# Two attentions on one core: GpSimd's third mask goes ahead of a subtraction, and the guarded add of the first attention moves into the next step

## The reference, cut to what matters

```
x = x + L0_attn(layernorm(x))            # 32 sequences of 256 tokens, 16 heads of 8, causal
x = x + L0_ffn(layernorm(x))             # routed experts
h = layernorm(x)                         # L1_attn, on the same tokens:
for l in range(4):
    xn = ln(h, ln1_w[l], ln1_b[l])
    q, k, v = heads(xn @ Wq.T + bq), heads(xn @ Wk.T + bk), heads(xn @ Wv.T + bv)
    scores = (q k^T + rel_shift((q + u) r^T)) * HEAD_DIM ** -0.5
    p = softmax(where(j > i, -inf, scores))
    h = h + (p v) @ Wo.T + bo
    h = h + gelu(ln(h) @ W1.T + b1) @ W2.T + b2
x = x + h
...                                      # top-2 experts, performer, fp4 feed-forward, one-head attention, adapters
```

## Time and profile before

| | |
|---|---|
| median of 3 runs | 6347.32 us (6344.32 to 6354.53) |
| profiled execution, its own time | 6347.19 us |
| its span | 6345.5 us |
| TensorE matmul, busy | 5660.9 us (89%) |
| VectorE, busy | 4069.9 us (64%) |
| ScalarE, busy | 2817.1 us (44%) |
| GpSimd, busy | 2118.2 us (33%) |

### The profile page before, as it was taken

The page is one execution under the profiler, slowest core; times in us unless marked ns, Lnnn a source line. Parts: engine busy times, 40 slices in busy tenths (PEclk is TensorE's granted clock), DMA queues, the critical chain, the costliest instruction groups (busy, mean ns, idle before and its releaser), DMA issues. The chain is left out here.

```text
span 6345.5 us, 121186 instructions
## 1 busy us (share of the span) xinstructions
PE 5660.9 (89%) x38029; PEld 3508.4 (55%) x38029; DVE 4069.9 (64%) x9572; ACT 2817.1 (44%) x4608; POOL 2118.2 (33%) x3000
## 2 busy tenths in 40 slices
PE   7997999999997999979987999889988989886677
PEld 5664444444443677457754777457754556644564
DVE  7885666666664777357744776367745756567854
ACT  4553222222221555535553555445554645543344
POOL 5551000000001666146632665156620012253322
PEclk9998999999998999989998999989999999997799
DMA  4332323222323555045522554055510000000002
GB/s 132 103 108 93 97 98 98 95 97 97 97 98 99 154 149 151 1 128 152 151 62 62 155 150 125 3 148 153 149 39 5 0 7 0 1 4 0 0 2 61
DMA packets 526328, 527.02 MB, mean 83 GB/s; under 512 B 55698, under 2 KB 436705, under 8 KB 503780
## 3 DMA queue, kind: packets, MB, share of 16 engines
q1 hardware_dynamic: 517684, 517.90, 29.3%
q10 hardware_dynamic: 8320, 5.25, 0.3%
HBM read 337.88 MB, written 185.07 MB: 82 GB/s over the span
## 5 line engine op out<-in xcount | busy, mean ns | idle before, releaser
L361 DVE TENSOR_REDUCE a_mx<-a_unit 128x2 f32<-128x512 f32 (+1 forms) x1920 | 1298.5, 688 | 611.7 <-PE a_unit L556 602.9
L460 ACT ACTIVATE a_prob<-a_slot 128x1536 f32<-128x1536 f32 x640 | 929.1, 1452 | 732.4 <-PE a_slot L579 577.7
L554 PE MATMUL a_unit<-a_sk,a_sq 96*128 96x256 bf16 (+3 forms) x5120 | 747.7, 250 | 87.9 <-DVE a_mx L361 44.3
L1169 ACT ACTIVATE f_silu<-f_pG 128x512 f32<-128x512 f32 x528 | 315.1, 598 | 934.4 <-PE f_pG L1244 920.4
L556 PE MATMUL a_unit<-a_maskq,identb 128*128 128x256 bf16 (+1 forms) x1920 | 602.5, 314 | 0.0
L1111 DVE TENSOR_TENSOR f_gated<-f_spread,f_silu 128x512 f32<-128x512 f32 x512 | 354.6, 693 | 348.2 <-ACT f_silu L1169 308.0
L1221 PE MATMUL f_pO<-f_hidden,f_wd 128*128 128x512 f32 x1056 | 545.0, 598 | 14.2 <-DVE f_hidden L1113 14.0
L554 PEld LDWEIGHTS a_unit<-a_sk,a_sq 96*128 96x128 bf16 (+1 forms) x5120 | 382.8, 99 | 291.2 <-DVE a_mx L361 161.3
L1244 PE MATMUL f_pG<-f_xnT,f_wg 128*128 128x512 f32 x1056 | 541.8, 595 | 0.0
L1248 PE MATMUL f_pU<-f_xnT,f_wu 128*128 128x512 f32 x1056 | 540.7, 594 | 0.0
L602 PE MATMUL a_pctx<-a_prob,a_vaug 128*32 128x256 f32 x5120 | 422.9, 391 | 90.9 <-POOL a_prob L307 86.7
(11 more groups left out here) (409 smaller groups left out, 11027.7 us busy)
## 6 DMA issues: line engine op xcount, KB each, us to landing
f_spread<-f_scratch SPq DMA_DIRECT2D x1024, 128.0 KB, 2.9
a_sq<-a_qscratch SPq DMA_DIRECT2D x128, 768.0 KB, 5.7
a_sk<-a_kscratch SPq DMA_DIRECT2D x160, 384.0 KB, 6.6
a_qscratch<-a_parts SPq DMA_DIRECT2D x288, 192.0 KB, 2.3
a_qscratch<-a_parts SPq DMA_DIRECT2D x288, 128.0 KB, 2.2
a_kscratch<-a_parts SPq DMA_DIRECT2D x160, 192.0 KB, 2.2
a_kscratch<-a_parts SPq DMA_DIRECT2D x160, 128.0 KB, 2.2
a_qscratch<-a_parts SPq DMA_DIRECT2D x288, 64.0 KB, 1.8
```

The costliest lines, as they stand in the source:

```text
L361: v.tensor_reduce(dst, src, op=ALU.max, axis=AX.X, negate=True).then_inc(red_done, 1)
L460: act.activation(prob[gr % 2][:, :], slot[:, :], ACT.Exp, scale=SCALE).then_inc(exp_done, 1)
L554: pe.matmul(bank[:, at * wide:(at + 1) * wide], q, sk[b][0:KM, gr * GH + h, 0:wide], start=(at == 0), stop=False)
L1169: act.activation(silu[c % 2][:, :], pG[c % 2][:, :], ACT.Silu).then_inc(silu_done, 1)
```

## The change

Three moves, none of which adds or removes work on data:

1. GpSimd, both attentions: the masks of the third head group (`causal(2)`) are issued between the first cast of the split and its subtraction, no longer between the subtraction and the second cast. One more semaphore increment (`apart`) stands in front of the subtraction.
2. GpSimd, first attention: the fill of `guard` goes from the start of the step to its end.
3. VectorE, first attention: the guarded add of sequence n-1 goes from the end of step n to step n+1, behind that step's fifth reduction (`units(3, 5)`), as `add_guarded(n - 2)`. The last one is done at the end of the last step.

```diff
@@ GpSimd
-                    if not rel and is_seq(n - 1):
-                        if is_seq(n - 2):
-                            g.wait_ge(op_taken, n - 1)
-                        g.tensor_tensor(guard[:, :, :], zeros[:, :, :], zeros[:, :, :], op=ALU.add).then_inc(guard_done, 1)
                     causal(0)
...
                         chain.link(g.tensor_copy(pt[:, :, 0, :], f32s[:, :, :]))
-                        chain.link(g.tensor_tensor(rest[:, :, :], f32s[:, :, :], pt[:, :, 0, :], op=ALU.subtract))
                     causal(2)
                     if is_seq(n + 4):
                         pt = parts[j % 2]
+                        g.sem_inc(apart, 1)
+                        chain.link(g.tensor_tensor(rest[:, :, :], f32s[:, :, :], pt[:, :, 0, :], op=ALU.subtract))
                         chain.link(g.tensor_copy(pt[:, :, 1, :], rest[:, :, :]))
                         g.tensor_tensor(pt[:, :, 2, :], rest[:, :, :], pt[:, :, 1, :], op=ALU.subtract
                                         ).then_inc(parts_done, 1)
+                    if not rel and is_seq(n - 1):
+                        if is_seq(n - 2):
+                            g.wait_ge(op_taken, n - 1)
+                        g.tensor_tensor(guard[:, :, :], zeros[:, :, :], zeros[:, :, :], op=ALU.add).then_inc(guard_done, 1)
@@ VectorE
+                def add_guarded(m):
+
+                    dst = rows(store, m * QT, QT)
+                    v.wait_ge(guard_done, m + 1)
+                    v.wait_ge(osb_done, m + 1)
+                    chain.link(v.tensor_tensor(isnum[:, :, :], osb[:, :, :], osb[:, :, :], op=ALU.is_equal))
+                    chain.link(v.copy_predicated(guard[:, :, :], isnum[:, :, :], osb[:, :, :]))
+                    v.tensor_tensor(dst, guard[:, :, :], dst, op=ALU.add).then_inc(op_taken, 1)
...
                     units(3, 5)
+                    if not rel and is_seq(n - 2):
+                        add_guarded(n - 2)
...
                     units(9, 12)
-                    if is_seq(n - 1):
+                    if rel and is_seq(n - 1):
                         dst = rows(store, (n - 1) * QT, QT)
-                        if rel:
-                            v.wait_ge(op_pe, n)
-                            got = ring[0][:, 0:SEQ].rearrange("p (t d) -> p t d", d=D)
-                        else:
-                            v.wait_ge(guard_done, n)
-                            v.wait_ge(osb_done, n)
-                            chain.link(v.tensor_tensor(isnum[:, :, :], osb[:, :, :], osb[:, :, :], op=ALU.is_equal))
-                            chain.link(v.copy_predicated(guard[:, :, :], isnum[:, :, :], osb[:, :, :]))
-                            got = guard[:, :, :]
+                        v.wait_ge(op_pe, n)
+                        got = ring[0][:, 0:SEQ].rearrange("p (t d) -> p t d", d=D)
                         v.tensor_tensor(dst, got, dst, op=ALU.add).then_inc(op_taken, 1)
+                    if not rel and once(n, SEQS):
+                        v.drain()
+                        add_guarded(n - 1)
```

## The result

The changed kernel takes 6261.98 us (median of 4 runs, 6256.44 to 6276.41) against 6347.75 of the kernel before, taken beside it: ratio 0.9873, 95% interval 0.986 to 0.9885. The forecast of 6286 had the sign and the main mechanism, and was 24 us too high. The profiled execution has a span of 6259.8 us.

The account below looks back on a forecast made before the run. TensorE was taken to set the pace in both attentions, so only its idle gaps could be won. From 6347.3, less 78 (relative attention) plus 17 (first attention), came 6286 us; range 6250 to 6338.

Parts of the forecast that it names:

- Relative attention, the wait for L307 gone: -78 us: Relative attention: TensorE's wait at values for GpSimd's second mask instruction goes, except in each layer's last four sequences; -78 us.
- L67 delayed to 1.8 us a pair, covered by 0.3 us: Relative attention: VectorE's L67 pair meets the moved subtraction, yet the reduction behind it is 0.3 us early; cost 0.
- Rivals 3 and 4: Relative attention: L67's second instruction waits for cast L336, 6336 us (12%); GpSimd starves VectorE, 6535 us (5%).
- SP's cover holds: Relative attention: SP's writes and loads behind `parts_done` still bring the stack in time for `maxima`; cover's thickness unknown.
- rival 5: Relative attention: a wait of `maxima` for the stack's loads replaces the one for L307; 6364 us, 6%.
- The added increment and the guard fill: 0: GpSimd: the extra semaphore increment costs next to nothing; first attention's guard fill goes to an idle stretch, 0 us.
- First attention, uncollided: -1 us, 0.52 of the 0.56 given back: First attention: without collision, the moved add ends one 0.56 us wait but delays L678, keeping 0.04 a step; -1 us.
- Collision: two of three instructions 0.33 us late each, +17 us: First attention: L432 and L434 of the moved add each meet a GpSimd mask, making L678 0.66 us later; +17 us.

Follow-up runs that it names:

- The add alone: The changed kernel with the old order on GpSimd, so only guard fill and guarded add are moved: 6340.31 us, ratio 0.9995 to the kernel before.

## Why the prediction was right, and where it was not

- *Relative attention, the wait for L307 gone: -78 us.* Right. Steps went from 15.95 to 15.19 us, the masks come 1.2 us early, and the order alone, in that attention alone, gives 6271.94 against 6341.34, -69 us with an interval of -62 to -81. From first to last context copy the four layers are 75 us shorter, in that kernel as in the changed one. What remains of the wait is 7.4 us in 16 instances, the four last sequences of each layer, as forecast (4 x 1.9).
- *L67 delayed to 1.8 us a pair, covered by 0.3 us.* Right, to 0.05 us. Rivals 3 and 4 did not come: the second L67 got in before the cast each time it is seen above.
- *SP's cover holds.* Right, but I could not size it. The masks ahead of the cast and the doubled subtraction show that 0.75 us more on that path costs 22 us and 1.7 us costs 93: rival 5 was near.
- *The added increment and the guard fill: 0.* Nothing in the traces speaks against it: L332, with the increment in front of it, starts at 2249.82, where L307 ends (2249.85), and none of VectorE's waits in the first attention ends with the fill.
- *First attention, uncollided: -1 us, 0.52 of the 0.56 given back.* The mechanism was right, and so was the place: the chain moved from one spot where TensorE waits for VectorE to another, and L686 follows L425 by 0.06 us in every step. From the third unit of the maxima to L686 the forecast's working gives 281.93 - 273.41 = 8.52 us without a collision (273.41 is 273.97 less 0.56); measured are 8.65, against 8.00 before. What came free at the step's start was 0.72, not 0.56, which the listed wait didn't show.
- *Collision: two of three instructions 0.33 us late each, +17 us.* This is the term that was mis-sized. The collision is real, on the two instructions that were named, but its price on VectorE's way to L678 was 0.15 us instead of 0.66: L370 and L371 took 0.40 us more together, and the gap of 0.19 that had stood between the add and the next reduction, at a step's start, is not there at the new place. GpSimd's masks lose too, 0.08 and 0.17 us, which the forecast left out; their loss makes a wait of TensorE that is over before the one for VectorE decides. Net: 0 in steady steps, instead of 0.62 a step. A part of this is luck, as 0.16 us more came free than was counted.
- *Not in the sum:* the first attention ends 4.8 us earlier. Its last context copy starts at 538.1 before and 533.3 after, though the steady steps are equal; in the last steps the split of the maxima (L387) had waited behind the add (TensorE's longest wait for it there was 2.0 us). The add alone shows it too (532.0), but not clearly in its time.

6347.3 less 75 (four layers, each 18 to 20 us shorter from first to last context copy) less 5 is 6267. Another 8.6 us are gone from the three stretches between a layer's last context copy and the next one's first (674.2 to 665.6), which hold the feed-forward and the emptying and filling of the pipeline. With only one half of the change they take 672; why both are needed stays open. Of the 24 us by which the forecast was too high, 17 are the collision's term and 5 the first attention's end.

## What to carry to other kernels

When an engine's queue has a wait in it, work belongs behind the masks or copies that another engine waits for, not in front; look whether it is covered today and whether it will still be when the step gets shorter. When a chain of instructions is moved on an engine, follow the engine from there to the next result that the bounding engine takes: on the way to L425 the chain gave back all that it had saved, and two reductions earlier nothing waited for it. When a wait has gone, look at the weight loads as well as the matmuls before saying which wait took its place. And a part that measures as worth nothing alone may be what makes the next one pay.

## What the runs showed of the hardware

- Instructions of VectorE and GpSimd on tiles in SBUF took longer beside each other, on both engines. Beside a three-instruction chain the two masks took 0.72 and 0.81 us instead of 0.64 and the cast behind them 0.79 instead of 0.61; beside a single add the first mask took 0.81 and the second 0.63. L369, started 0.2 us before L306, kept its 0.41, and L370, started 0.29 us behind L306, took 0.73 for 0.46. L306 ran on for 0.43 us behind L370's start, and L370 lost 0.27 of them.
- Beside a subtraction of GpSimd (1.65 us, to 2251.47) the first of two L67 took 1.59 us, to 2251.55, and the pair 1.85 for 0.60, while the reductions from PSUM beside GpSimd's cast and second subtraction took 0.68 and 0.69; all 238 reductions from 2100 to 2400 us took between 0.67 and 0.69.
- A matmul wait of 1.2 us in twenty steps stood beside one of 8.0 us for the same result at the weight load (L686).
- From 2100 to 2400 us, in the relative attention's first layer, TensorE had 300.00 of 300 us of modelled busy time at a granted clock of 1.00. Over all four layers, 2010 to 4680 us, the granted clock was 0.96, before the change and after it.
